# One-core attention, FFN and scan kernel: startup in order of need, weight tasks moved in the first FFN step, rope's turned half in PSUM, identity transposes ahead of the first input

## The chip, the core and the metric

The kernel runs on one core of a Trainium2 chip. The core has a matrix engine (TensorE, here PE; loading its stationary operand is listed apart, as PEld), VectorE (DVE), ScalarE (ACT), GpSimd (POOL) and a queue engine for transfers (SyncE, SP). They run side by side and wait for each other through semaphores. SBUF is the working memory; PE writes its results to PSUM, eight banks of 128 x 512 floats. The metric is the device time in microseconds, the median of several runs.

## What is computed

x is 4 x 512 x 256 floats. Four residual layers follow each other, each on the layer norm of x:

```
x = x + attention(layernorm(x))     # latent attention, 16 heads, causal
x = x + ffn(layernorm(x))
x = x + scan(layernorm(x))          # linear recurrence over 512 steps
x = x + ffn(layernorm(x))           # the same weights again

attention: q_c = rms(x @ wq_down.T) * q_norm_w         # 192 wide
           kv_c = rms(x @ wkv_down.T) * kv_norm_w      # 64 wide
           q = [q_c @ wq_up.T, rope(q_c @ wq_rope.T)]  # 128 + 64 per head
           k = [(kv_c @ wkv_up.T)[:128], rope(x @ wk_rope.T)]
           out = softmax(mask(q k.T * scale)) @ v @ wo.T
rope:      o1 = x1*cos - x2*sin;  o2 = x1*sin + x2*cos
ffn:       w = lut[idx]  (16 values);  down(silu(gate(x)) * up(x))
scan:      xp = x @ W_in.T; dt = softplus(xp @ W_dt.T + b); y_t = exp(-dt*exp(log_A)) * y_(t-1) + xp_t
```

## The kernel before

Every engine has its own program, written out by hand; there is no scheduler. Matrices that need full precision are split into a high and a low part (`_hi`, `_lo`), and a product is three matmuls (`split_mm`, L615 to L617). ACT writes the high part of a PSUM bank, DVE the low part.

*Weight tasks.* `TASKS` is a list of small steps (semaphore to wait for, count, functions for PE, ACT and DVE, PSUM bank). `pe_tasks`, `act_tasks` and `dve_tasks` run a range of it; a task's bank is free when DVE is done with its last user. D tasks transpose the `down` weights, N tasks multiply `wqu` by `wkn` into `wa`/`wb` (this folds the up projection of q with that of k, L294), R tasks transpose the rope weights into the same tensors (L306), W tasks transpose `wo` (L316), V tasks multiply it by the value weights into `wo_a`/`wo_b` (L373; "v-output tasks"), G tasks transpose the FFN's gate and up weights, S and the last L task prepare the scan's weights, the first three L tasks transpose `w_dn`. POOL builds the FFN weights from the 16-value table in chunks of `GC` columns, one comparison (L746) and one addition (L752) for each value, and raises `lut_sum`.

*Startup (batch 0).* DVE takes the statistics of x, normalises it to `xn`; PE transposes it (L580); `down` projects it per tile of 128 tokens; ACT copies each tile to `cd` and takes squares (`down_copy`, L778, L784); DVE runs `token_step` 0 to 23: root of the mean square, scaling of q (L1061), scaling of kv, rope of k. `to_features` (L1444) transposes `cd` in three blocks (q's first 128 columns, its last 64, and k), which ACT and DVE split (`feature_high`, `feature_low`).

*Attention loop.* A unit is four heads of one tile of 128 queries, 16 units a batch, 64 in all. Work is pipelined in slots: slot s runs `q_up` of unit s (L1459 to L1463, bank 0), `q_transpose` of unit s-2, scores of units s-2 and s-3, transposes of probabilities and products with values of s-4 and s-5, and the output projection of s-6. On DVE, `rope_q` of unit s reads bank 0: the product with cos goes to `q_tok` (L1111), the turned half times sin to `q_rot` (L1113, L1114), and L1116 adds them. The first 8 slots (`LEAD`) of batch 0 have nothing of an earlier batch beside them; W and V tasks follow slots 0 to 2 there (`early_tasks`), and after slot 1 DVE takes the statistics of batches 1 to 3 (`at_stats_of`) and normalises batch 1.

*FFN and scan.* Eight steps of 512 tokens follow (each batch once for each FFN layer); the first (`pe_first`, `act_first`, `dve_first`) has the remaining weight tasks between its gate/up tiles.

## Time and profile before

| | |
|---|---|
| Median of 3 runs | 856.2 us (856.1 to 857.96) |
| Profiled execution | 857.25 us, span 855.2 us |
| Busy share of the span | PE 89%, PEld 76%, DVE 79%, ACT 71%, POOL 59% |
| Chain that ended last | PE 59%, DVE 15%, ACT 12%, issue 12% |
| PE clock by 1/40 of the span | full, but for slices 2 and 4 (0.7 and 0.6) and slice 30 (0.8) |

A row of the timeline gives start, duration, engine, line, tiles and, in brackets, the idle time before it and what ended it. Matmul durations overlap: the distance between starts is the rate. The granted clock is 1.00 at 2.4 GHz and 0.50 at 1.2 GHz. Busy shares are means over stages with different limits, so stages are read one by one.

### The profile page before, as it was taken

How to read it: one execution, taken by the hardware profiler on the slowest of the kernel's cores; microseconds unless marked ns; L12 is line 12 of the kernel's file. 1: busy time of each engine (PE TensorE's matmuls, PEld its weight loads, DVE VectorE, ACT ScalarE, POOL GpSimd, SP SyncE). 2: the span in 40 equal slices, each digit the busy share in tenths (PEclk: the TensorE clock that was granted, in tenths of full speed). 3: DMA queues.
4: the chain of work that ended last, by engine and by line, in shares of the span. 5: the costliest groups of instructions: out<-in, count | busy, mean ns of one | idle time of the engine just before them, and what ended most of it. 6: DMA issues, size and time to landing. Idle time of an engine off the chain costs nothing.

```text
span 855.2 us, 15308 instructions
## 1 busy us (share of the span) xinstructions
PE 763.8 (89%) x4556; PEld 652.6 (76%) x4556; DVE 677.6 (79%) x2216; ACT 610.7 (71%) x1500; POOL 503.2 (59%) x543
## 2 busy tenths in 40 slices
PE   4767988898989899998899999999898999999998
PEld 3656767787877687876777888877787887887987
DVE  3676879898879999888989899896756778777643
ACT  2455888888888888888888899996515575665232
POOL 0599999999999999999999999981000000000000
PEclk9796999999999999999999999999989999999999
DMA  9800000000000000000000100000000000000000
GB/s 245 256 1 1 1 1 2 1 2 2 2 1 2 1 1 2 2 1 2 1 2 1 38 2 1 2 1 1 1 1 1 1 1 2 1 1 25 26 26 25
DMA packets 15377, 14.53 MB, mean 17 GB/s; under 512 B 5792, under 2 KB 14432, under 8 KB 15040
## 3 DMA queue, kind: packets, MB, share of 16 engines
q1 hardware_dynamic: 13792, 11.41, 4.6%
q0 software_dynamic: 624, 2.12, 0.8%
q8 instruction: 37, 0.61, 0.3%
q14 instruction: 44, 0.36, 0.1%
q10 hardware_dynamic: 880, 0.04, 0.1%
HBM read 11.46 MB, written 2.10 MB: 16 GB/s over the span
## 4 chain that ended last, share of the span: by engine, by line
PE 59%; DVE 15%; ACT 12%; issue 12%; DMA 0%; DVEq 0%; SPq 0%; ACTq 0%
PE bank L615 12%; PE bank L617 11%; PE bank L616 11%; PE bank L1496 4%; ACT prob L798 4%; ACT prob L818 3%; PE bank L1510 2%; PE bank L1513 2%; DVE pt_lo L1149 2%; ACT pt_hi L827 2%; PE bank L1523 2%; PE bank L580 2%; PE bank L1525 2%; DVE bias_m L1097 1%; PE bank L1470 1%
## 5 line engine op out<-in xcount | busy, mean ns | idle before, releaser
L746 POOL TENSOR_SCALAR hot<-raw_gu,lut 128x256 f32<-128x256 int32 x165 | 192.9, 1169 | 16.7
L752 POOL TENSOR_TENSOR total<-total,hot 128x256 f32<-128x256 f32 (+1 forms) x238 | 172.9, 726 | 19.9
L1097 DVE CUSTOM_DVE_ANT_0 bank<-bank,mask 128x128 f32<-128x128 f32 (+3 forms) x256 | 126.1, 493 | 38.6 <-issue 36.5
L798 ACT ACTIVATE prob<-bank,bias_m 128x128 f32<-128x128 f32 (+3 forms) x256 | 136.1, 532 | 23.9 <-DVE bias_m L1097 23.2
L1149 DVE TENSOR_TENSOR pt_lo<-bank,pt_hi 128x512 fp32r<-128x512 f32 x160 | 108.9, 681 | 10.2 <-ACT pt_hi L827 10.0
L1496 PE MATMUL bank<-ident,prob 128*128 128x128 f32 x640 | 98.6, 277 | 14.9 <-ACT prob L818 10.3
L818 ACT ACTIVATE prob<-prob,rden 128x128 f32<-128x128 f32 (+3 forms) x224 | 105.4, 536 | 6.0 <-DVE rden L1132 5.5
L615 PE MATMUL bank<-kt_hi,qt_hi 128*128 128x128 f32 (+3 forms) x256 | 89.6, 350 | 19.8 <-DVE xt_lo L589 5.0
L827 ACT CAST pt_hi<-bank 128x512 fp32r<-128x512 f32 x160 | 93.5, 585 | 13.9 <-PE bank L1513 8.8
L746 POOL TENSOR_SCALAR hot<-raw_dn,lut 128x256 f32<-128x256 int32 (+1 forms) x90 | 97.2, 1080 | 9.1
L1496 PEld LDWEIGHTS bank<-ident,prob 128*128 128x128 f32 x640 | 72.9, 140 | 31.9 <-ACT prob L818 16.7
L616 PE MATMUL bank<-kt_lo,qt_hi 128*128 128x128 f32 (+3 forms) x256 | 83.1, 325 | 0.0
L617 PE MATMUL bank<-kt_hi,qt_lo 128*128 128x128 f32 (+3 forms) x256 | 83.1, 324 | 0.0
L615 PEld LDWEIGHTS bank<-kt_hi,qt_hi 128*128 128x128 f32 x256 | 48.9, 191 | 35.7 <-DVE xt_lo L589 7.7
L1510 PE MATMUL bank<-pt_hi,v_hl 128*128 128x512 f32 x160 | 68.6, 429 | 5.1 <-issue 4.3
L901 ACT ACTIVATE silu<-bank 128x512 f32<-128x512 f32 x40 | 24.0, 601 | 67.1 <-PE bank L617 67.1
L615 PE MATMUL bank<-xt_hi,gu_hi 128*128 128x512 f32 (+1 forms) x176 | 70.2, 399 | 1.5 <-DVE h_f L1269 1.5
L617 PE MATMUL bank<-xt_hi,gu_lo 128*128 128x512 f32 (+1 forms) x176 | 69.4, 394 | 0.0
L616 PE MATMUL bank<-xt_lo,gu_hi 128*128 128x512 f32 (+1 forms) x176 | 69.3, 394 | 0.0
L1523 PE MATMUL bank<-wo_a,o_a 128*128 128x256 f32 x256 | 68.2, 299 | 0.1
L1525 PE MATMUL bank<-wo_b,o_b 128*128 128x256 f32 x256 | 63.7, 281 | 0.0
L1513 PE MATMUL bank<-pt_lo,v_hl 128*128 128x512 f32 x160 | 63.2, 395 | 0.3 <-DVE pt_lo L1149 0.2
(207 smaller groups left out, 2103.0 us busy)
## 6 DMA issues: line engine op xcount, KB each, us to landing
x<-in_L_attn_a_x_dram SPq DMA_DIRECT2D x4, 512.0 KB, 7.3
wo_nat<-in_L_attn_a_wo_dram SPq DMA_DIRECT2D x1, 2048.0 KB, 13.6
out_dram<-x SPq DMA_DIRECT2D x16, 128.0 KB, 1.8
wqu<-in_L_attn_a_wq_up_dram SPq DMA_DIRECT2D x2, 768.0 KB, 9.0
wqr<-in_L_attn_a_wq_rope_dram SPq DMA_DIRECT2D x4, 192.0 KB, 7.3
raw_dn<-in_L_ffn_down_idx_dram POOLq DMA_DIRECT2D x1, 688.0 KB, 10.1
raw_gu<-in_L_ffn_gate_idx_dram POOLq DMA_DIRECT2D x1, 640.0 KB, 7.4
raw_gu<-in_L_ffn_up_idx_dram POOLq DMA_DIRECT2D x1, 640.0 KB, 7.9
```

Source lines behind the costliest of these rows:

```text
L615: nc.tensor.matmul(o, l_hi, r_hi, start=start and k == 0, stop=False)
L616: nc.tensor.matmul(o, l_hi, r_lo, start=False, stop=False)
L617: last = nc.tensor.matmul(o, l_lo, r_hi, start=False, stop=stop and k == n - 1)
L746: nc.gpsimd.tensor_scalar((hot if v else total)[:, 0:n], raw[:, c:c + n], float(v), lut[:, v:v + 1], ALU.is_equal, ALU.mult).then_inc(lut_ ...
L752: nc.gpsimd.tensor_tensor(dst, total[:, 0:n], hot[:, 0:n], ALU.add).then_inc(lut_sum, 1)
L798: nc.scalar.activation(prob[:, n % 2, h, 0:w], bank[2 + h % 2][:, 0:w], ACT.Exp, bias=bias_m[:, n % 2, h:h + 1], scale=-1.0, accum_out=den ...
L818: nc.scalar.activation(prob[:, n % 2, h, 0:w], prob[:, n % 2, h, 0:w], ACT.Copy, scale=rden[:, n % 2, h:h + 1]).then_inc(norm_a, 1)
L827: nc.scalar.copy(pt_hi[:, c % 2, :, :].rearrange("p h d -> p (h d)"), bank[4 + c % 2][:, :])\
L1097: nc.vector.tensor_tensor_reduce(out=bank[2 + h % 2][:, 0:w], in0=bank[2 + h % 2][:, 0:w], in1=mask[:, TB * P - w:TB * P], scale=1.0, scal ...
L1149: nc.vector.tensor_tensor(pt_lo[:, c % 2, :, :].rearrange("p h d -> p (h d)"), bank[4 + c % 2][:, :], pt_hi[:, c % 2, :, :].rearrange("p h ...
L1496: last = nc.tensor.transpose(bank[4 + c % 2][:, h * P:(h + 1) * P], prob[:, n % 2, h, j * P:(j + 1) * P], ident[:, :])
L1510: nc.tensor.matmul(bank[6][:, :], v, pt_hi[:, c % 2, :, :].rearrange("p h d -> p (h d)"), start=j == 0, stop=False)
```

## The change

- PE transposes the identity 32 times into bank 0 while it waits for `xn`, and 8 times after the D tasks.
- The N and R tasks are ordered by half: the four that heads 0 to 7 need, then (after slot 0's `q_up`) the other four. All four `down` tiles come before them. The first two feature blocks are made before the kv scaling and the rope of k.
- The statistics of batches 1 to 3 are dealt out behind the V tasks (12 `bn_stats`), in slot 3 (aggregation and root) and in slot 4 (normalisation). The transposes of `xn` of batch 1 move to slots 4 and 5, bank 7.
- `q_rot` is gone from SBUF: the turned half is written over the first 64 columns of each head in bank 0. `q_up` waits for all four operations of the unit before it, not for three.
- `GC` is 352 columns in place of 256.
- In the first FFN step the `w_dn` tasks come before the scan's; the last scan task (`t_dt_in`) is run inside `ffn_down`, between its two pairs of tiles.

```diff
+WARM = 32
...
-        GC = GT * DIM // 11
+        GC = GT * DIM // 8
...
+        R_TASKS = [(qr_dup, 1, t_rope(p, k), 4 + p) for k in range(2) for p in range(2)]
+        Q_TASKS = N_TASKS[0:2] + R_TASKS[0:2] + N_TASKS[2:4] + R_TASKS[2:4]
...
+        L_TASKS = [(lut_sum, gu_sums + dn_sums, t_dn(k), 4 + k) for k in range(3)]
+        S_TASKS = [(ssm_in, 64, t_wdt(), 7), (ssm_in, 64, t_ssm(0), 2), (ssm_in, 64, t_ssm(2), 3),
+                   (ssm_in, 64, t_dt_in(), 2)]
+        TASKS = D_TASKS + Q_TASKS + W_TASKS + V_TASKS + G_TASKS + L_TASKS + S_TASKS
...
+        def rest_stats(k):
+            e, tiles = nc.vector, slice(TB, BATCH * TB)
+            if k < REST_TILES:
+                if k % TB == 0:
+                    e.wait_ge(x_in_s[1 + k // TB], 16)
+                e.bn_stats(at_stats[:, TB + k, :], x[:, TB + k, :]).then_inc(at_bn, 1)
+            elif k == REST_TILES:
+                e.wait_ge(at_bn, BATCH * TB)
+                settle(2 * G)
+                for t in range(TB, BATCH * TB):
+                    e.bn_aggr(at_mv[:, t, :], at_stats[:, t, :]).then_inc(at_agg, 1)
+                e.wait_ge(at_agg, BATCH * TB)
+                e.tensor_scalar(at_v[:, tiles], at_mv[:, tiles, 1], LN_EPS, None, ALU.add).then_inc(at_ref, 1)
+            else:
+                rsqrt_step(k - REST_TILES - 1, at_ref, RSQRT + 2, at_v[:, tiles], at_r[:, tiles], at_t[:, tiles])
         def at_norm(p, t):
...
+                turned = heads(bank[0])[:, :, 0:KR]
...
-                nc.vector.tensor_tensor(q_rot[:, :, 0:half], raw[:, :, half:ROPE], s0, ALU.mult).then_inc(q_rope, 1)
-                nc.vector.tensor_tensor(q_rot[:, :, half:ROPE], raw[:, :, 0:half], s1, ALU.mult).then_inc(q_rope, 1)
+                nc.vector.tensor_tensor(turned[:, :, 0:half], raw[:, :, half:ROPE], s0, ALU.mult).then_inc(q_rope, 1)
+                nc.vector.tensor_tensor(turned[:, :, half:ROPE], raw[:, :, 0:half], s1, ALU.mult).then_inc(q_rope, 1)
                 dve.wait_ge(q_rope, k + 3)
-                nc.vector.tensor_tensor(q, q, q_rot[:, :, :], ALU.add).then_inc(q_rope, 1)
+                nc.vector.tensor_tensor(q, turned, q, ALU.add).then_inc(q_rope, 1)
...
+            def early_dve(k0, k1):
+                for k in range(k0, k1):
+                    dve_tasks(dve, k, k + 1)
+                    if V0 <= k < G0:
+                        for j in range(REST_TILES * (k - V0) // (G0 - V0), REST_TILES * (k + 1 - V0) // (G0 - V0)):
+                            rest_stats(j)
...
+                    if b == 0 and s == 3 and k <= RSQRT:
+                        rest_stats(REST_TILES + k)
+                    if b == 0 and s == 4 and k < TB:
+                        at_norm(1, k)
+                    if b == 0 and s in (4, 5) and k == 11:
+                        dve_xt_part(1, s - 4, bank[7])
...
+            for k in range(1 + RSQRT + TB):
+                token_step(k, 0)
             dve.wait_ge(qn_ready, 2)
-            dve_tasks(dve, N0, N0 + 2)
+            dve_tasks(dve, N0, N1)
+            feature_low(0, 0)
+            feature_low(0, 1)
             dve.wait_ge(tables_in, 16 * 3)
-            for k in range(TOKEN_STEPS):
+            for k in range(1 + RSQRT + TB, TOKEN_STEPS):
                 token_step(k, 0)
-            dve_tasks(dve, N0 + 2, W0)
-            for k in range(3):
-                feature_low(0, k)
+            dve_slot(0, 0, None, (N1, W0))
+            feature_low(0, 2)
             split_values(0)
             dve.wait_ge(a_exp, 1)
             nc.vector.tensor_scalar(a_neg[:, :], a_neg[:, :], -1.0, None, ALU.mult).then_inc(a_ready, 1)
-            for s in range(LEAD):
+            early_dve(*early_tasks(0))
+            for s in range(1, LEAD):
                 dve_slot(s, 0, None, early_tasks(s))
-                if s == 1:
-                    for b in range(1, BATCH):
-                        dve.wait_ge(x_in_s[b], 16)
-                    at_stats_of(1, BATCH)
-                    for t in range(TB):
-                        at_norm(1, t)
-                if s == 3:
-                    dve_xt(1)
             for b in range(BATCH - 1):
                 for s in range(LEAD, UNITS + LEAD):
                     dve_slot(s, b, b + 1)
...
             pe.wait_ge(ident_in, 16)
+            for k in range(WARM):
+                nc.tensor.transpose(bank[0][:, k % 4 * P:(k % 4 + 1) * P], ident[:, :], ident[:, :])
             pe_xt(0)
             pe_tasks(pe, D0, N0)
+            for k in range(WARM // 4):
+                nc.tensor.transpose(bank[0][:, k % 4 * P:(k % 4 + 1) * P], ident[:, :], ident[:, :])
             def down(b, t):
...
-                free_after(pe, q_rope, 4 * (b * UNITS + n) - 1)
+                free_after(pe, q_rope, 4 * (b * UNITS + n))
...
-            down(0, 0)
-            down(0, 1)
-            pe_tasks(pe, N0, N0 + 1)
-            for t in (2, 3):
-                pe.wait_ge(dp_cp, t - 1)
+            for t in range(TB):
+                if t >= 2:
+                    pe.wait_ge(dp_cp, t - 1)
                 down(0, t)
-            pe_tasks(pe, N0 + 1, W0)
-            pe.wait_ge(prep_act, W0)
-            pe.wait_ge(prep_dve, W0)
-            pe.wait_ge(sq, 2 * TB)
+            pe_tasks(pe, N0, N1)
+            pe.wait_ge(prep_act, N1)
+            pe.wait_ge(prep_dve, N1)
+            pe.wait_ge(tok, 1 + TB)
+            to_features(0, 0)
+            to_features(0, 1)
+            pe_slot(0, 0, None)
+            pe_tasks(pe, N1, W0)
             pe.wait_ge(tok, 1 + 12)
-            for k in range(3):
-                to_features(0, k)
-            for s in range(LEAD):
-                if s == 5:
-                    wait_xt(pe, 1)
+            to_features(0, 2)
+            pe_tasks(pe, *early_tasks(0))
+            for s in range(1, LEAD):
+                if s == 2:
+                    pe.wait_ge(prep_act, W0)
+                    pe.wait_ge(prep_dve, W0)
                 if s == 6:
                     pe.wait_ge(prep_act, G0)
                     pe.wait_ge(prep_dve, G0)
                 pe_slot(s, 0, None)
                 pe_tasks(pe, *early_tasks(s))
-                if s == 3:
+                if s == 4:
                     pe.wait_ge(prep_dve, G0)
-                    pe_xt(1)
+                if s in (4, 5):
...
-            def ffn_down(k, si):
+            def ffn_down(k, si, inside=None):
                 for pair in range(0, TB, 2):
+                    if pair and inside is not None:
+                        inside()
                     if pair and si is not None:
                         pe.wait_ge(sp_act, 4 * si + 2)
...
-                pe_tasks(pe, G0 + 4, S0)
+                pe_tasks(pe, G0 + 4, L0)
                 weights(G0 + 4)
                 gate_up(0, 2)
                 gate_up(0, 3)
-                pe_tasks(pe, S0, S0 + 2)
-                weights(S0)
+                pe_tasks(pe, L0, L0 + 2)
+                weights(L0)
                 gate_up(0, 4)
-                pe_tasks(pe, S0 + 2, L0 + 1)
+                pe_tasks(pe, L0 + 2, S0 + 1)
                 gate_up(0, 5)
-                pe_tasks(pe, L0 + 1, L1)
-                weights(L0 + 3)
+                weights(L0 + 2)
                 pe_xt(ffn_xt(1))
-                weights(L1)
-                ffn_down(0, None)
+                pe.wait_ge(hf_s, FT)
+                pe_tasks(pe, S0 + 1, S1 - 1)
+                weights(S0 + 1)
+                ffn_down(0, None, lambda: pe_tasks(pe, S1 - 1, S1))
             pe_first()
+            weights(S1)
             for k in range(1, STEPS):
```

ACT's program is reordered in the same way. The transfers and their order are unchanged.

Line numbers in the rows of the changed kernel are its own; there `down` is L635 to L637, `to_features` L1482, `q_up` L1497 to L1501, the xn transposes L600.

PE's program at startup, before, from the last `down` matmul on (`wkn`, `wqu`: N tasks; `wqr`: R tasks; `cd`: `to_features`; `wo_nat`: W tasks):

```order
L617 MATMUL bank<-down_hi,xt_lo 128x320
L294 MATMUL bank<-wkn,wqu 128x64 x24
L306 MATMUL bank<-ident,wqr 128x128 x16
L1444 MATMUL bank<-ident,cd 128x128 x4
L1444 MATMUL bank<-ident,cd 64x128 x4
L1444 MATMUL bank<-ident,cd 128x128 x4
L1459 MATMUL bank<-wa_hi,qa_hi 128x512
L1460 MATMUL bank<-wa_lo,qa_hi 128x512
L1461 MATMUL bank<-wa_hi,qa_lo 128x512
```

and in the changed kernel, from its last `down` matmul on:

```order
L637 MATMUL bank<-down_hi,xt_lo 128x320
L294 MATMUL bank<-wkn,wqu 128x64 x16
L306 MATMUL bank<-ident,wqr 128x128 x8
L1482 MATMUL bank<-ident,cd 128x128 x4
L1482 MATMUL bank<-ident,cd 64x128 x4
L1497 MATMUL bank<-wa_hi,qa_hi 128x512
L1498 MATMUL bank<-wa_lo,qa_hi 128x512
L1499 MATMUL bank<-wa_hi,qa_lo 128x512
L1500 MATMUL bank<-wb_hi,qb_hl 128x512
L1501 MATMUL bank<-wb_lo,qb_hl 128x512
L294 MATMUL bank<-wkn,wqu 128x64 x16
L306 MATMUL bank<-ident,wqr 128x128 x8
```

The first `q_up` (five matmuls with `wa` and `wb`) has moved ahead of half of the N and R tasks and of the third feature block.

DVE's program at the V tasks (`wo_b`: the V tasks' low part; `at_stats`: statistics of batches 1 to 3; `qt_lo`: unit 0), before:

```order
L383 TENSOR_TENSOR wo_b<-bank,wo_a 64x512 x3
L1121 TENSOR_TENSOR qt_lo<-bank,qt_hi 128x512
L524 BN_STATS at_stats<-x 128x6 x12
L498 MEMSET scratch 128x1
L528 BN_AGGR at_mv<-at_stats 128x2 x12
L531 TENSOR_SCALAR at_v<-at_mv 128x12
L507 TENSOR_SCALAR at_t<-at_v 128x12
L509 TENSOR_SCALAR at_r<-at_t 128x12
```

and in the changed kernel:

```order
L383 TENSOR_TENSOR wo_b<-bank,wo_a 64x512
L544 BN_STATS at_stats<-x 128x6
L383 TENSOR_TENSOR wo_b<-bank,wo_a 64x512
L544 BN_STATS at_stats<-x 128x6 x2
L383 TENSOR_TENSOR wo_b<-bank,wo_a 64x512
L544 BN_STATS at_stats<-x 128x6
L1142 TENSOR_TENSOR qt_lo<-bank,qt_hi 128x512
L383 TENSOR_TENSOR wo_b<-bank,wo_a 64x512
L544 BN_STATS at_stats<-x 128x6 x2
L383 TENSOR_TENSOR wo_b<-bank,wo_a 64x512
L544 BN_STATS at_stats<-x 128x6
L383 TENSOR_TENSOR wo_b<-bank,wo_a 64x512
```

The twelve statistics stood in one piece behind three of the eight V tasks; now one or two stand behind each.

PE's program at the end of the first FFN step, from the last matmul of the last gate/up tile (112 rows) on (`w_dn`: the L tasks; `wdt_t`: `t_dt_in`; `xn`: the next step's input; `dn_hi`, `h_hi`: `ffn_down`), before:

```order
L617 MATMUL bank<-xt_hi,gu_lo 112x512
L414 MATMUL bank<-ident,w_dn 128x128 x6
L414 MATMUL bank<-ident,w_dn 48x128 x2
L363 MATMUL bank<-wdt_t,ssm_nat 128x256 x4
L580 MATMUL bank<-ident,xn 128x128 x8
L615 MATMUL bank<-dn_hi,h_hi 128x256
L616 MATMUL bank<-dn_lo,h_hi 128x256
```

and in the changed kernel:

```order
L637 MATMUL bank<-xt_hi,gu_lo 112x512
L600 MATMUL bank<-ident,xn 128x128 x8
L331 MATMUL bank<-ident,ssm_nat 128x128 x8
L635 MATMUL bank<-dn_hi,h_hi 128x256
L636 MATMUL bank<-dn_lo,h_hi 128x256
L637 MATMUL bank<-dn_hi,h_lo 128x256
```

The `w_dn` transposes have gone from here to earlier gate/up tiles, the input of the next step stands right behind the last tile, and `t_dt_in` is no longer ahead of `ffn_down`.

## Rows read from the trace of the kernel before

**Rows 1.** stretches: us; busy us of PE, PEld, DVE, ACT, POOL (instructions); clock, DMA, GB/s

```profile
80.00:592.00 512.00, 466.07 (x2876) 395.02 (x2875) 452.63 (x1576) 445.35 (x1203) 456.28 (x487) 1.00 0.01 3
592.00:633.00 41.00, 36.95 (x215) 32.53 (x214) 25.65 (x65) 17.57 (x33) 0.00 (x0) 0.92 0.00 1
```

**Rows 2.** a DMA issue, then the timeline to 50 us: start, us, engine, line, tiles

```profile
ident<-in_ident_dram SPq DMA_DIRECT2D x1, 64.0 KB, 1.8
...
10.90 1.94 PE L580 MATMUL bank<-ident,xn 128*128 128x128 f32 x8 [10.90 <-DVE xn L543]
...
15.61 0.60 PE L615 MATMUL bank<-down_hi,xt_hi 128*128 128x320 f32 x1 [1.13 <-DVE down_lo L275]
...
23.55 0.41 ACT L778 COPY cd<-bank 128x320 f32<-128x320 f32 x1
...
24.64 0.19 ACT L784 ACTIVATION_READ_ACCUMULATOR squares<-cd 128x1 f32 x1
...
26.35 0.16 DVE L1056 TENSOR_SCALAR rms_v<-ms 128x8 f32<-128x8 f32 x1
...
28.81 1.01 DVE L1061 TENSOR_SCALAR cd<-cd,rms_r 128x192 f32<-128x192 f32 x4
...
31.84 0.74 DVE L283 SCALAR_TENSOR_TENSOR wa_lo<-bank,qn_a,wa_hi 128x512 fp32r<-128x512 f32 x1
...
35.98 2.79 PE L1444 MATMUL bank<-ident,cd 128*128 128x128 f32 x12 [1.80 <-issue]
...
39.40 0.76 PE L1459 MATMUL bank<-wa_hi,qa_hi 128*128 128x512 f32 x1 [0.62 <-ACT kt_hi L791]
...
49.37 2.83 PE L373 MATMUL bank<-wo_t,wv 128*128 128x256 f32 x12 [1.77 <-DVE wo_t L324]
```

**Rows 3.** a stretch of one microsecond, and the timeline of PE in it

```profile
43.00:44.00 1.00, 1.00 (x7) 1.00 (x6) 0.89 (x3) 0.51 (x2) 0.90 (x2) 0.52 0.00 0
...
41.67 3.90 PE L316 MATMUL bank<-ident,wo_nat 128*128 128x128 f32 x24
```

**Rows 4.** timeline, 55 to 73 us, DVE, ACT and PE

```profile
55.34 4.01 DVE L524 BATCH_NORM_STATS2 at_stats<-x 128x6 f32<-128x256 f32 x12
...
57.00 0.59 ACT L379 CAST wo_a<-bank 128x512 fp32r<-128x512 f32 x1 [2.02 <-PE bank L373]
...
66.00 2.47 DVE L383 TENSOR_TENSOR wo_b<-bank,wo_a 64x512 fp32r<-64x512 f32 x4
...
70.11 0.68 DVE L383 TENSOR_TENSOR wo_b<-bank,wo_a 64x512 fp32r<-64x512 f32 x1 [1.65 <-ACT wo_b L380]
...
72.32 0.73 PE L1459 MATMUL bank<-wa_hi,qa_hi 128*128 128x512 f32 x1
```

**Rows 5.** who waited for `q_rot`; the addition's durations and group; two pairs of the timeline

```profile
  PE bank L1459: 2.3, 7
...
L1116 DVE TENSOR_TENSOR q_tok<-q_tok,q_rot x64: 424/426/992, 43.2 to 562.3; 128x256 f32<-128x256 f32 x64
...
L1116 DVE TENSOR_TENSOR q_tok<-q_tok,q_rot 128x256 f32<-128x256 f32 x64 | 33.0, 516 | 2.2
...
84.77 0.28 DVE L1114 TENSOR_TENSOR q_rot<-bank,sin 128x128 f32<-128x128 f32 x1
...
85.20 0.47 PE L1459 MATMUL bank<-wa_hi,qa_hi 128*128 128x512 f32 x1
...
497.82 0.28 DVE L1114 TENSOR_TENSOR q_rot<-bank,sin 128x128 f32<-128x128 f32 x1
...
498.25 0.47 PE L1459 MATMUL bank<-wa_hi,qa_hi 128*128 128x512 f32 x1
```

**Rows 6.** timeline of PE, 618 to 628 us, idle time before in brackets

```profile
618.89 1.06 PE L580 MATMUL bank<-ident,xn 128*128 128x128 f32 x8 [1.82 <-issue]
...
621.71 0.55 PE L615 MATMUL bank<-dn_hi,h_hi 128*128 128x256 f32 x1 [1.75 <-issue]
...
627.61 0.30 PE L615 MATMUL bank<-dn_hi,h_hi 128*128 128x256 f32 x1
```

97 lines of the change are left out of this document (48 added, 49 removed).

## The prediction

> **What bounds the kernel now.** I read the stretches first, then the timeline of the two where TensorE (PE) is not full, then the waits around `q_up` in the attention loop. In the long attention part, 80 to 592 us, PE is busy 466 of 512 us and VectorE (DVE) 453, ScalarE (ACT) 445: three engines near full that hand work round a loop [rows 1]. So a saved microsecond of PE alone is worth little there, and a longer step in the loop can cost all of itself. Outside the loop it is different: the first FFN step (592 to 633) has PE busy 37 of 41 us, with waits in one place [rows 1, 6], and before 80 us each engine waits for the others in turn [rows 2 to 4].
>
> **The change part by part.** The profiled execution took 857.25 us (span 855.2, 2.05 around it); the median of the plain runs is 856.2. I sum against 857.25 and take 1.05 off at the end.
>
> *Prologue order, up to the first v-output task.* Before, the first `q_up` starts at 39.40, because the feature transposes (35.98) wait until all eight `wa`/`wb` tasks and the whole token chain are through DVE [rows 2]. After, they wait for four tasks and for the first half of the token chain. Built from durations of the rows: the PE clock is assumed up when x is normalised (below), so the first `down` starts at about 14.1 in place of 15.61 (14 transposes of 1.94 us per eight, half of it saved, less what ACT's copies keep). All four `down` tiles follow each other, and ACT paces them: one tile is 23.55 to 24.83, 1.28 us. First tile ready at 15.1, so the squares end at 15.1 + 4 x 1.28 = 20.2 (before 24.83). DVE then does the 12 small steps and four scalings, 26.35 to 29.82, that is 3.5 us: 23.7. Four `wa`/`wb` halves at 0.74 us each, overlapping to 0.66: 26.4. `to_features` for two of three blocks, and from its start to the first `q_up` 39.40 - 35.98 = 3.4: 29.9. That is 9.5 us earlier. What was deferred now lies between this `q_up` and the first v-output task (49.37): before that took 10.0 us; the four further `wa`/`wb` tasks and their matmuls add the 2.7 us of DVE and about 0.9 us in which PE and ACT fill the pipe: 13.6, so 43.5. Term: 43.5 - 49.37 = **-5.9**. DVE, and not PE, is the engine that is late here. The transfers do not stop it: by 43 us nothing is moved any more [rows 3], and the spread statistics read x from about 44 on.
>
> *Statistics of batches 1 to 3 spread out.* Before, DVE runs 12 `BATCH_NORM_STATS2` (55.34, 4.01 us) and then aggregates, takes the root and normalises until 66.0, 10.7 us in one piece, while its `wo_b` splits wait, and DVE finishes the last split at 70.11 + 0.68 = 70.79 [rows 4]. From 49.37 that is 21.4 us. After, the stats are interleaved with the eight tasks. ACT then paces: two casts of 0.59 us each per task, 8 x 1.2 = 9.6, with a `qt_hi` and a `q_tok` copy between them (1.0), PE's lead before the first cast (about 1.1) and one last split (0.7): 12.4 us. A stat and a half beside each split is 0.6 + 0.6 us of DVE in 1.2 us of ACT, so it is hidden; if not, it would cost up to 4.0. Term: **-9.0**. The other 66.0 - 59.35 = 6.7 us of DVE work comes back in slots 3 and 4, where `rest_stats` and `at_norm` sit between the parts. DVE had room there before, since PE ran slow (a `q_up` matmul took 0.73 us at 72.32, against 0.47 at 85.20 [rows 4, 5]). Bounds 0 and 6.7; I take **+1.9**, as DVE work per slot and the room nearly balance in slot 3 and not in slot 4. Prologue in all: -13.0, with bounds of -17 and -8.
>
> *Warm transposes.* The identity lands about 2.9 us in (issue at 0.72 plus 0.38, 1.8 to land), and eight cold transposes take 1.94 us, so 32 take at most 7.8 us and end by 10.7, before PE's first input at 10.90 [rows 2]. At about 43.98 the clock rose from 1.2 to 2.4 GHz when PE had been running a `q_up` and then transposes without pause since 39.40, and the last 2.1 us of that were transposes of `wo_nat` [rows 2, 3]. I read that as transposes counting as activity. The eight after the `down` weight tasks are then about 0.9 us beside ACT's and DVE's splits. Against it: the transposes of xn and of the `down` weights ran from 10.90 to 14.48 (1.13 before 15.61) and the first `down` matmul still took 0.60. If the clock doesn't rise, `down` starts at 14.48 + 8 x 0.24 = 16.4 instead of 14.1, and its tiles are paced by PE at 1.6 us (six matmuls 0.27 apart): 16.4 + 6.4 + 1.3 = 24.1, 3.9 later. The Trainium skill, "TensorE: Matmul & The Clock Gate", part 4 on PE-mode transposes, says that a transpose doesn't count as PE-busy in the same way and that the full clock doesn't engage for it; by that rule the warm transposes are idle load and this second case is the one that comes about. The trace has a row for either reading.
>
> *Rope's turned half in PSUM.* The last addition reads PSUM and SBUF instead of two SBUF tiles. Its 64 instances took 33.0 us, 516 ns on average, while the shortest took 424, which I take as the price without interference: at best 64 x 0.09 = 5.9 us of DVE less [rows 5]. But the halves now stand in bank 0, so `q_up` of the next unit must wait for the fourth operation and not for the third. DVE is just ahead of PE there: the second half ends at 85.05 and `q_up` starts at 85.20; at 498.10 and 498.25 the same 0.15 us. Of the 59 units from unit 5 on, 36 start within 0.35 us of that end; these two are the first and the last of them [rows 5]. The addition ends about 0.46 us after it, so these `q_up` come up to 0.45 us later. Full price 36 x 0.45 = 16.2 us; gain if none passes -5.9. The trace puts only 2.3 us over 7 times down to this wait [rows 5]; yet the chain of waits, followed through these slots, runs over `q_up` in about half of them. Half of the first (8) less half of the second (3): **+5**. Behind the waiting `q_up` on PE stand the scores of head 3, which DVE's last row maximum and ACT's exp wait for.
>
> *Larger chunks on GpSimd (256 to 352 columns).* GpSimd's table sums were done before the first FFN step (GpSimd is busy 0.00 us in 592 to 633 [rows 1]), so nobody waits for them. Fewer, longer instructions end earlier and leave DVE undisturbed at the end: **-1**, between -3 and +1.
>
> *First FFN step.* PE waits 1.82 us before the transposes of xn (618.89) and 1.75 us before `ffn_down` (621.71), because `dn_lo` and the last `ssm_lo` come late on DVE. After that pause the clock is at 1.2 GHz until 627.61: 27 matmuls in 5.90 us, that is 0.22 us each, and about 0.12 at 2.4 GHz [rows 6]. After, the `w_dn` tasks stand two gate tiles earlier, xn follows the last gate tile without a wait, and the `wdt`-times-`w_in` task, before `ffn_down` so far, stands inside it, with the same work. Gain 1.82 + 1.75 - 0.2 for a shorter wait on `h_f`, and 2.6 for the slow stretch: **-6.0**, between -3.4 (clock drops all the same) and -7. PE sets the pace after that, so it stays. Late next is `h_f` of the last tile.
>
> Sum: -13.0 - 6.0 + 5 - 1 = -15.0. 857.25 - 15.0 - 1.05 = 841.2, so 841 us.
>
> **Rivals.**
> 1. *The rope wait is absorbed.* For it: the trace books only 2.3 us to it, and DVE saves up to 5.9. Against it: PE and DVE are both near 90% busy, so there is little slack. Then the term is -3 in place of +5: 833.
> 2. *The clock doesn't rise on transposes.* The prologue gives 3.9 us less: 845. For it: after 3.6 us of transposes the first `down` matmul ran slow. Against: the rise during `wo_nat`'s transposes. (This is where the rule of the Trainium skill named above leads.)
> 3. *DVE is the bound of slots 3 to 5.* All 6.7 us come back, and the stats aren't hidden (4.0): 841 + 4.8 + 4.0 = 850. For it: DVE has the work in either order. Against: while PE waited for it in the old block, ACT and PE were the ones idle, and with the block gone DVE gets their time.
> 4. *Slower than before.* The mechanism is the q_up wait alone. If each of the 64 units is lengthened, by the wait for the addition and by slower writes to PSUM, the gains elsewhere (20.0 us) are used up from 20.0 / 64 = 0.31 us a unit on. At 0.45 us the term is 64 x 0.45 = 29, and the time 856.2 - 20.0 + 29 = 865. Against it: 23 of 59 units have more than 0.35 us to spare, and DVE's part gets shorter.
>
> **How the numbers follow.** Forecast (838 to 844) 0.44; rival 1 0.22; rival 2 0.15; rival 3 0.12; rival 4 0.04; something that leaves the time where it is, 0.03. The range reaches from a rope gain with a full prologue, 830, to rival 3, 850; outside it lie about 2 in 10. A measurement tells about 0.2% (1.7 us) from no change. Faster by more: 0.93; within: 0.03; slower: 0.04.
>
> **What the profile would show.** Right: the first `q_up` near 30 and the first v-output matmul near 43; no PE pause of 7 us between v-output tasks; `ffn_down` straight behind the transposes with the clock at full level; `q_up` starting some 0.15 us after the addition in most units, and the stretch between the eighth unit and the last scores about 4 us longer. Wrong: `down` not before 16 and its matmuls 0.27 us apart, as at 1.2 GHz; slots 3 and 4 longer than 7.5 us each; an unchanged or shorter attention loop, which would say that the wait is absorbed.

## The result and the profile after

The changed kernel takes 867.2 us (median of 4 runs, 865.55 to 869.07) against 856.15 us before: a ratio of 1.013, 95% interval 1.010 to 1.016. It is slower; the forecast was 841 us, 830 to 850. A few executions lay far outside the others of the same kernel (885.76, 2376.35, 2546.01 and 4090.15 us); they are in no ratio.

First the page of the changed kernel, busy tenths and granted clock in 40 slices:

```profile
span 865.5 us, 15232 instructions
PE   7777988898888898898899899999998999999998
PEclk9695999999999999999999999999999999999999
```

Then the two long stretches, the attention loop and the first FFN step (us; busy us of PE, PEld, DVE, ACT, POOL; clock, DMA, GB/s), to be read beside [rows 1]:

```profile
80.00:605.00 525.00, 469.04 (x2866) 395.29 (x2865) 452.08 (x1572) 445.49 (x1199) 409.83 (x340) 0.99 0.01 3
605.00:645.00 40.00, 37.98 (x229) 32.26 (x229) 28.40 (x70) 18.66 (x35) 0.00 (x0) 1.00 0.00 1
```

The loop does the same work (469 us of PE, 452 of DVE) in 525 us in place of 512. The FFN step runs wholly at 2.4 GHz now, 0.92 before. The clock's row shows the startup at 0.6 and 0.5 in slices 2 and 4, where the kernel before has 0.7 and 0.6. In slice 1 the row is no guide: it reads full in the kernel before, although `down`'s first twelve matmuls start 0.27 us apart there (15.61 to 18.68) and its last twelve 0.15 us (21.18 to 22.88). Up to the first change that the row shows, the durations tell the clock.

The timeline of PE to 51 us (start, us, engine, line, tiles, wait before it), for [rows 2]:

```profile
2.91 6.59 PE L1463 MATMUL bank<-ident 128*128 128x128 f32 x32 [2.91 <-DMA ident<-in_ident_dram]
...
10.96 1.09 PE L600 MATMUL bank<-ident,xn 128*128 128x128 f32 x8 [1.46 <-DVE xn L563]
...
14.50 0.38 PE L635 MATMUL bank<-down_hi,xt_hi 128*128 128x320 f32 x1 [0.43 <-DVE down_lo L275]
...
27.44 1.94 PE L1482 MATMUL bank<-ident,cd 128*128 128x128 f32 x8 [4.58 <-DVE wb_lo L283]
30.85 0.76 PE L1497 MATMUL bank<-wa_hi,qa_hi 128*128 128x512 f32 x1 [1.48 <-DVE qb_hl L1109]
...
33.12 6.92 PE L294 MATMUL bank<-wkn,wqu 128*128 128x64 f32 x32
39.84 1.91 PE L306 MATMUL bank<-ident,wqr 128*128 128x128 f32 x8
...
50.18 2.83 PE L373 MATMUL bank<-wo_t,wv 128*128 128x256 f32 x12 [1.78 <-DVE wo_t L324]
```

Up to the first `q_up` the forecast holds: `down` at 14.50 (forecast 14.1), feature transposes 27.44 (26.4), `q_up` 30.85 (29.9), 8.6 us earlier than before. Then everything is lost. From this `q_up` to the first v-output matmul it is 19.3 us, where the forecast had 13.6 and the kernel before 10.0. The four deferred tasks' 32 matmuls take 6.92 us, 0.22 us each, where the same kind took 0.114 before. The eight feature transposes took 1.94 us, the level of 1.2 GHz, and stand behind a wait of 4.58 us. The first v-output task starts at 50.18, 0.8 us later than before.

The same kernel in the V tasks and slots 3 to 5 (timeline of PE and DVE), for [rows 4]:

```profile
55.93 0.67 DVE L1142 TENSOR_TENSOR qt_lo<-bank,qt_hi 128x512 fp32r<-128x512 f32 x1
...
56.70 0.45 PE L635 MATMUL bank<-kt_hi,qt_hi 128*128 128x128 f32 x1 [2.08 <-issue]
...
57.37 5.86 PE L373 MATMUL bank<-wo_t,wv 128*128 128x256 f32 x20
...
67.66 0.48 PE L635 MATMUL bank<-kt_hi,qt_hi 128*128 128x128 f32 x1 [3.69 <-ACT prob L818]
...
77.42 0.77 PE L1497 MATMUL bank<-wa_hi,qa_hi 128*128 128x512 f32 x1 [1.21 <-DVE q_tok L1137]
...
80.76 1.38 DVE L563 TENSOR_SCALAR xn<-x,at_mv,at_r 128x256 f32<-128x256 f32 x3
...
87.16 0.54 PE L1497 MATMUL bank<-wa_hi,qa_hi 128*128 128x512 f32 x1
```

No 7 us pause is left, but there are pauses of 2.08 us (1.73 at the same place before) and 3.69 us, and the `q_up` at 77.42 still has matmuls of 0.77 us. The granted clock is 0.50 from 68 to 86 us; in the kernel before it was from 66 to 78. Starts of `q_up` by unit (from the timelines):

| unit | before | after |
|---|---|---|
| 0 | 39.40 | 30.85 |
| 3 | 72.32 | 68.65 |
| 5 | 85.20 | 87.16 |
| 8 | 102.04 | 104.86 |
| 63 | 553.69 | 571.35 |

So 2.8 us are lost by unit 8, and 14.8 us between units 8 and 63 (466.49 us against 451.65). What lies behind unit 63 is 7.4 us shorter.

A timeline is one execution, and startups differ. In six timelines with the same order of the startup and no warm transposes (the kernel before and five of the runs below) the first `q_up` starts between 39.30 and 42.04 and the first v-output matmul between 49.23 and 51.62. Differences of 2 us at the start of a single timeline are therefore not evidence by themselves.

Rope in the changed kernel, for [rows 5]: who waited (us in total, times, longest), and the group of the addition (count, busy us, mean ns, idle before):

```profile
PE bank L1497 <- DVE q_tok L1137: 14.5, 31, 1.5
```

```profile
L1137 DVE TENSOR_TENSOR q_tok<-bank,q_tok 128x256 f32<-128x256 f32 x64 | 27.2, 425 | 2.2
```

The addition got as short as forecast (33.0 us to 27.2), and the wait for it went from 2.3 us over 7 times to 14.5 over 31.

The end of the first FFN step, for [rows 6]:

```profile
630.90 1.03 PE L600 MATMUL bank<-ident,xn 128*128 128x128 f32 x8
633.27 1.09 PE L331 MATMUL bank<-ident,ssm_nat 128*128 128x128 f32 x8 [1.34 <-DVE h_f L1300]
634.12 0.36 PE L635 MATMUL bank<-dn_hi,h_hi 128*128 128x256 f32 x1
```

The wait before xn is gone, one of 1.34 us (for `h_f`, "late next" in the prediction) is left, and `ffn_down` runs at 0.12 us a matmul from its start.

### The profile page after: what moved, and what is told of

The parts are those of the page before. It is cut to its first block, busy times and chain, and to the rows that moved or that the text cites. A ratio compares the mean times of both kernels' runs of the same rounds, so it can differ in the third digit from the quotient of the medians.

```text
span 865.5 us, 15232 instructions
## 1 busy us (share of the span) xinstructions
PE 775.4 (90%) x4596; PEld 659.3 (76%) x4596; DVE 677.8 (78%) x2216; ACT 611.7 (71%) x1500; POOL 458.3 (53%) x388
## 4 chain that ended last, share of the span: by engine, by line
PE 56%; DVE 18%; issue 14%; ACT 11%; DMA 0%; DVEq 0%; SPq 0%; ACTq 0%
PE bank L635 11%; PE bank L637 11%; PE bank L636 10%; PE bank L1534 4%; ACT prob L838 3%; DVE pt_lo L1170 3%; ACT prob L818 2%; PE bank L1548 2%; PE bank L1551 2%; PE bank L1563 2%; DVE bias_m L1117 2%; PE bank L1565 2%; PE bank L1497 2%; DVE o_b L1176 2%; ACT pt_hi L847 1%
## 5 line engine op out<-in xcount | busy, mean ns | idle before, releaser
L766 POOL TENSOR_SCALAR hot<-raw_gu,lut 128x352 f32<-128x352 int32 x120 | 176.6, 1472 | 12.2
L772 POOL TENSOR_TENSOR total<-total,hot 128x352 f32<-128x352 f32 (+1 forms) x168 | 157.7, 938 | 14.0
L635 PE MATMUL bank<-kt_hi,qt_hi 128*128 128x128 f32 (+3 forms) x256 | 90.1, 352 | 22.3 <-DVE xt_lo L609 5.3
L766 POOL TENSOR_SCALAR hot<-raw_dn,lut 128x352 f32<-128x352 int32 (+1 forms) x60 | 87.0, 1450 | 6.1
L637 PE MATMUL bank<-kt_hi,qt_lo 128*128 128x128 f32 (+3 forms) x256 | 83.8, 327 | 0.0
L635 PEld LDWEIGHTS bank<-kt_hi,qt_hi 128*128 128x128 f32 x256 | 49.4, 193 | 38.2 <-DVE xt_lo L609 8.0
L635 PE MATMUL bank<-xt_hi,gu_hi 128*128 128x512 f32 (+1 forms) x176 | 70.2, 399 | 1.6 <-DVE h_f L1300 1.5
L637 PE MATMUL bank<-xt_hi,gu_lo 128*128 128x512 f32 (+1 forms) x176 | 69.4, 394 | 0.0
## 6 DMA issues: line engine op xcount, KB each, us to landing
wo_nat<-in_L_attn_a_wo_dram SPq DMA_DIRECT2D x1, 2048.0 KB, 12.4
```

The costliest lines, as they stand in the source:

```text
L635: nc.tensor.matmul(o, l_hi, r_hi, start=start and k == 0, stop=False)
L637: last = nc.tensor.matmul(o, l_lo, r_hi, start=False, stop=stop and k == n - 1)
L766: nc.gpsimd.tensor_scalar((hot if v else total)[:, 0:n], raw[:, c:c + n], float(v), lut[:, v:v + 1], ALU.is_equal, ALU.mult).then_inc(lut_ ...
L772: nc.gpsimd.tensor_tensor(dst, total[:, 0:n], hot[:, 0:n], ALU.add).then_inc(lut_sum, 1)
```

## The experiments

Each ratio is against the kernel before, timed beside it on the same chip, with a 95% interval; "us" is the ratio less one times 855. Theory at this point: rope's wait costs its full price in the loop, and the prologue's gain is given back because TensorE falls to 1.2 GHz in its waits. Rivals: the parts cost something by themselves (GpSimd's chunks, PSUM writes), or deferred tasks are slow for another reason.

### Rope alone, and its wait alone

```diff
-                nc.vector.tensor_tensor(q, q, q_rot[:, :, :], ALU.add).then_inc(q_rope, 1)
+                nc.vector.tensor_tensor(q, turned, q, ALU.add).then_inc(q_rope, 1)
...
-                free_after(pe, q_rope, 4 * (b * UNITS + n) - 1)
+                free_after(pe, q_rope, 4 * (b * UNITS + n))
```

> The kernel before with rope's turned half in bank 0 (and q_up waiting for the fourth rope operation), nothing else. Theory A (the chain of the loop runs over q_up in nearly every unit, so the extra operation between the last read of bank 0 and q_up costs its 0.3 us a unit in full): the changed kernel's stretch from unit 8 to unit 63 was 466.5 us against 451.65, so here too 13 to 17 us more, 869 to 873 us. Rival B (my forecast's term, half of it absorbed): +5, 861 us. Rival C (the longer loop of the changed kernel comes from another part of the change, such as GpSimd's longer instructions): 856 to 858 us.

Measured 866.74 us, ratio 1.0135 (1.0112 to 1.0159): +11.5 us. Theory A, a little below its range. The loop from unit 8 to 63 took 463.8 us, against 451.65. Its waits, and one pair of its timeline:

```profile
PE bank L1460 <- DVE q_tok L1117: 13.9, 33, 1.0
```

```profile
85.10 0.42 DVE L1117 TENSOR_TENSOR q_tok<-bank,q_tok 128x256 f32<-128x256 f32 x1
...
85.67 0.47 PE L1460 MATMUL bank<-wa_hi,qa_hi 128*128 128x512 f32 x1 [0.40 <-DVE q_tok L1117]
```

The same `q_up` started at 85.20 in [rows 5]: 0.47 us later, 0.15 us behind the addition's end, as forecast.

```diff
-                free_after(pe, q_rope, 4 * (b * UNITS + n) - 1)
+                free_after(pe, q_rope, 4 * (b * UNITS + n))
```

> The kernel before, with q_rot in SBUF as it was; only q_up waits for the fourth rope operation in place of the third. It tells the wait from the place of the operands. Theory A (the wait is the whole cost): the same as with the turned half in PSUM or slightly above it, since the addition here takes 516 ns on average and there 424: 869 to 877 us. Rival B (the wait is absorbed, the PSUM operand or writes cost the time): 856 to 859 us.

Measured 869.04 to 871.75 us, ratio 1.0175 (1.0149 to 1.0200): +15.0 us. There is no timeline of it to read. The wait is the whole cost. The PSUM operand by itself gives some 3.5 us back (15.0 less 11.5; the two intervals overlap), which is what the addition's 5.8 us of DVE were worth, less whatever the writes to PSUM cost.

### The changed kernel without rope

```diff
-                nc.vector.tensor_tensor(q, turned, q, ALU.add).then_inc(q_rope, 1)
+                nc.vector.tensor_tensor(q, q, q_rot[:, :, :], ALU.add).then_inc(q_rope, 1)
...
-                free_after(pe, q_rope, 4 * (b * UNITS + n))
+                free_after(pe, q_rope, 4 * (b * UNITS + n) - 1)
```

> The changed kernel with the rope part undone (q_rot in SBUF, at the end of the region, q_up waits for the third operation), chunks of 352 columns kept. Theory A: 867.2 less 13 to 17 us: 850 to 854 us, because the first FFN step's gain (7.4 us in the trace) is then no longer covered and the prologue's net is about +2. Rival B (rope is worth 5): 862 us. Rival C (the longer loop is not rope's): 866 to 868 us.

Measured 857.05 us, ratio 1.0027 (0.9999 to 1.0055). Against the changed kernel's 1.0130 that is 8.8 us less. Its loop took 453.5 us in an execution of 853.38 us, 3.7 under the run's median, so the loop of a median execution may well be longer. The run missed the expected 850 to 854: without rope the rest of the change does not gain either. Something beside rope costs some 4 us more than I had it.

### The first FFN step alone

> The kernel before with only the order of the first FFN step changed (w_dn tasks earlier, the input transposes straight behind the last gate tile, the wdt task inside ffn_down). Theory A (this term was right, the two traces differ by 7.4 us behind unit 63, of which some 1 us is GpSimd's): 6 to 7.5 us faster, 849 to 850 us. Rival B (the gain behind unit 63 comes mostly from GpSimd's larger chunks, which end earlier): 2 us or less, 854 to 856 us.

(Its edit is the part of the change's diff from `L_TASKS` on that concerns the first FFN step, in all three engines.) Measured 850.88 us, ratio 0.9951 (0.9932 to 0.9970): -4.2 us. Its timeline shows the same two things as the changed kernel's, xn without a wait and `ffn_down` at full clock:

```profile
616.67 1.09 PE L331 MATMUL bank<-ident,ssm_nat 128*128 128x128 f32 x8 [1.31 <-DVE h_f L1268]
617.51 0.36 PE L615 MATMUL bank<-dn_hi,h_hi 128*128 128x256 f32 x1
```

From the last `q_up` to the second input transposes it is 87.2 us in the kernel before, 85.6 in the rope-alone run (the same FFN code; there the slow clock behind the pause lasted 3.1 us, not 5.9), 81.6 here and 81.1 in the changed kernel. The other timelines agree: 85.6 to 87.2 us in the seven with the old order of this step, 81.0 to 82.0 in the nine with the new one. So the gain is 4 to 6 us, depending on how long the slow clock would have lasted.

### The three parts of the prologue, each alone

Warm transposes:

```diff
             pe.wait_ge(ident_in, 16)
+            for k in range(WARM):
+                nc.tensor.transpose(bank[0][:, k % 4 * P:(k % 4 + 1) * P], ident[:, :], ident[:, :])
             pe_xt(0)
             pe_tasks(pe, D0, N0)
+            for k in range(WARM // 4):
+                nc.tensor.transpose(bank[0][:, k % 4 * P:(k % 4 + 1) * P], ident[:, :], ident[:, :])
```

> The kernel before with only the identity transposes on TensorE added (32 ahead of its first input, 8 behind the down weights). The changed kernel's trace shows full clock for the first xn transposes (1.09 us for eight, 1.94 before). If that is what the transposes do by themselves: xn transposes from 10.9 at full clock, first `down` near 14.5 in place of 15.6, and then at most 1.1 us, since ScalarE's copies and VectorE's token chain pace what follows: 854 to 855.5 us. Rival (the Trainium skill, 'TensorE: Matmul & The Clock Gate', part 4, by which transposes leave the clock low): eight more cold transposes ahead of `down`, 0.8 to 2 us later: 856 to 858 us.

Measured 853.49 us, ratio 0.9979 (0.9956 to 1.0002): -1.8 us, an interval that just takes in no change.

```profile
11.02 1.34 PE L581 MATMUL bank<-ident,xn 128*128 128x128 f32 x8 [1.92 <-DVE xn L544]
...
15.35 0.39 PE L616 MATMUL bank<-down_hi,xt_hi 128*128 128x320 f32 x1
...
47.60 2.83 PE L374 MATMUL bank<-wo_t,wv 128*128 128x256 f32 x12 [1.77 <-DVE wo_t L325]
```

The transposes raised the clock: `down` runs at 0.31 us a matmul at once (0.47 without them, from a first one of 0.60 in [rows 2]). In between the clock had fallen once more: PE stood idle for 1.92 us ahead of the xn transposes, of which the last ran at half rate, the six of `dn_nat` took 1.84 us (1.16 in the changed kernel), and the granted clock is 0.50 in 12 to 14 us. The eight transposes behind them then brought it back. The first v-output task comes 1.8 us earlier, more than the 1.1 us I allowed.

Statistics spread over the V tasks (on VectorE; TensorE and ScalarE take the next input's transposes in slots 4 and 5):

```diff
-                if s == 1:
...
-                    at_stats_of(1, BATCH)
-                    for t in range(TB):
-                        at_norm(1, t)
+                    if b == 0 and s == 3 and k <= RSQRT:
+                        rest_stats(REST_TILES + k)
+                    if b == 0 and s == 4 and k < TB:
+                        at_norm(1, k)
```

> The kernel before with only the statistics and the normalisation of the next batches spread over the v-output tasks and slots 3 to 5. Theory A (the work comes back in slots 3 to 5, where VectorE and the slow clock decide, as in the changed kernel, whose q_up of units 3 to 8 come at 68.65, 77.42, 87.16 to 104.86 against 72.32, 79.70, 85.20 to 102.04): fourth q_up 3 to 5 us earlier, that of unit 8 within 1.5 us of 102.0; 855 to 857 us. Rival B (my forecast, -9.0 + 1.9): 848 to 850 us. Rival C (it costs by itself what the changed prologue loses): 858 to 860 us.

Measured 855.29 us, ratio 0.9995 (0.9970 to 1.0020): -0.4 us. The `q_up` of units 3, 4, 5 and 8:

```profile
66.28 0.73 PE L1483 MATMUL bank<-wa_hi,qa_hi 128*128 128x512 f32 x1
...
74.54 0.76 PE L1483 MATMUL bank<-wa_hi,qa_hi 128*128 128x512 f32 x1 [0.74 <-DVE q_rot L1132]
...
83.49 0.73 PE L1483 MATMUL bank<-wa_hi,qa_hi 128*128 128x512 f32 x1
...
101.25 0.40 PE L1483 MATMUL bank<-wa_hi,qa_hi 128*128 128x512 f32 x1
```

Unit 3 is 6.0 us earlier than the 72.32 of before, unit 8 only 0.8. The gain is real and comes back in slots 3 to 5, of which 3 and 4 take 8.3 and 9.0 us (7.4 and 5.5 before), at matmuls of 0.73 to 0.76 us (1.2 GHz). Theory A, with more gained by unit 3 than its 3 to 5 us.

The V tasks themselves, from their first matmul to VectorE's last split, took 14.7 us (49.40 to 64.09), where the forecast had 12.4 and the kernel before 21.4. The difference is a wait that [rows 4] did not make visible: PE stands 2.09 us before unit 0's scores (1.73 in the kernel before), and ScalarE's casts behind it stand 2.38.

The order up to the first v-output task:

```diff
-            pe_tasks(pe, N0 + 1, W0)
...
+            pe_tasks(pe, N0, N1)
...
+            to_features(0, 0)
+            to_features(0, 1)
+            pe_slot(0, 0, None)
+            pe_tasks(pe, N1, W0)
```

> The kernel before with only the order up to the first v-output task changed (four down tiles first, four wa/wb tasks, two feature blocks, the first q_up, then the other four tasks). Theory A (the four deferred tasks run at 1.2 GHz, 6.92 us for 32 matmuls in the changed kernel against 0.114 us each at 2.4 GHz before, so what the first q_up gains is lost again before the first v-output task): first q_up near 32, first v-output matmul 50 to 52, and 856 to 858.5 us. Rival B (my forecast's -5.9 less what the warm clock was worth in it): 850 to 853 us.

Measured 855.16 us, ratio 1.0002 (0.9977 to 1.0026): +0.2 us.

```profile
33.13 0.77 PE L1466 MATMUL bank<-wa_hi,qa_hi 128*128 128x512 f32 x1 [1.48 <-DVE qb_hl L1092]
...
35.40 6.92 PE L294 MATMUL bank<-wkn,wqu 128*128 128x64 f32 x32
...
52.79 2.83 PE L373 MATMUL bank<-wo_t,wv 128*128 128x256 f32 x12 [2.34 <-DVE wo_t L324]
```

The first `q_up` is 6.3 us earlier, the first v-output task 3.4 us later, and the 6.92 us are there again without the warm transposes. The median is a little below theory A's 856 to 858.5 and above rival B's 850 to 853; the profiled execution has it as A says. Of the 3.4 us, up to 2.3 can be the spread of startups (49.23 to 51.62 with the old order).

### GpSimd's chunks

```diff
-        GC = GT * DIM // 11
+        GC = GT * DIM // 8
```

The changed kernel with 256 columns (`// 11`):

> The changed kernel with GpSimd's chunks at 256 columns as before. It gives the price of the larger chunks within the change. Theory A (nobody waits for GpSimd; VectorE's additions beside it are 0.42 us in either case now that the addition reads PSUM): 867 to 868.5 us, 1 us at most above the changed kernel. Rival B (chunks of 352 hold VectorE up longer and are part of the loop's growth): 862 to 865 us.

Measured 864.46 us, ratio 1.0103 (1.0071 to 1.0136), against the changed kernel's 1.0130: 2.3 us less (the intervals overlap), loop 463.7 against 466.5. Rival B's side. And the kernel before with 352 columns:

> The kernel before with only GpSimd's chunks at 352 columns. With and without rope, going back to 256 columns made the changed kernel faster: ratio 1.0130 to 1.0103, and 1.0027 to 0.9978. Theory A (longer GpSimd instructions hold VectorE's SBUF operations up for longer, and the loop pays): 1 to 3 us slower, 856 to 858 us, the loop from unit 8 to 63 1.5 to 2.5 us longer than 451.65. Rival B (my forecast's -1; the two differences were scatter): 853.5 to 855.5 us.

Measured 861.04 us, ratio 1.0065 (1.0036 to 1.0095): +5.6 us, beyond theory A's 3. In its profiled execution unit 8 comes 1.9 us later, which is within the spread of startups, and the loop takes 455.2 us, 3.6 more. DVE is busy for 405.5 us of it, in place of 400.5, with the same work. Groups of DVE in 105 to 540 us (count, busy us, mean ns, idle before), of the kernel before and then of this one:

```profile
L1061 DVE TENSOR_SCALAR cd<-cd,rms_r 128x192 f32<-128x192 f32 x12 | 4.6, 384 | 0.1
...
L515 DVE SCALAR_TENSOR_TENSOR rms_r<-rms_t,rms_r 128x8 f32<-128x8 f32 x9 | 2.7, 301 | 0.0
...
L513 DVE SCALAR_TENSOR_TENSOR rms_t<-rms_t,rms_v 128x8 f32<-128x8 f32 x9 | 1.6, 177 | 0.1
```

```profile
L1061 DVE TENSOR_SCALAR cd<-cd,rms_r 128x192 f32<-128x192 f32 x12 | 5.5, 462 | 0.1
...
L513 DVE SCALAR_TENSOR_TENSOR rms_t<-rms_t,rms_v 128x8 f32<-128x8 f32 x9 | 3.6, 402 | 0.1
...
L515 DVE SCALAR_TENSOR_TENSOR rms_r<-rms_t,rms_r 128x8 f32<-128x8 f32 x9 | 2.5, 276 | 0.0
```

One operation on 8 columns that reads two SBUF tiles (L513) takes 402 ns on average in place of 177, and once 922 ns; the longest rope addition went from 0.99 to 1.22 us. GpSimd's own instructions are 1488 and 946 ns long in place of 1171 and 749. Such DVE work seems to stand until the GpSimd instruction ends, and a longer one holds it longer. The other timelines confirm L513 (341 to 402 ns in the three with 352 columns, 162 to 285 in the thirteen with 256), but not every operation: L515, of the same kind and size, takes 276 in place of 301, and L1061's 384 to 462 lies close to what timelines with 256 columns reach (416). So single operations are a weak measure here; the sum over the loop (5.0 us more) is the better one.

By the Trainium skill, "SBUF — State Buffer", section "Who interferes with whom", the two engines share a port pair which whoever starts first keeps for its whole instruction, and an operation with two SBUF inputs wants it too; the rows of L513 and of the addition agree, that of L515 shows no effect. That this holding is what lengthens the loop is argued from them, not shown by a run of its own. Against it stands that without rope the loop is no longer with 352 columns (453.5 us, in an execution faster than its median) than with 256 (453.8, in the next section).

### The prologue's parts together, and the clock held up

Prologue and FFN step alone are left when the changed kernel is taken without rope and with 256 columns:

> The changed kernel without its rope part and without the larger GpSimd chunks: prologue and first FFN step alone. Parts measured by themselves: FFN -4.2, warm transposes -1.5, spread +0.3, order +0.2. Theory A (the prologue's parts disturb each other: at unit 8 the changed kernel is 2.1 to 2.8 us late, the parts alone sum to -0.8): FFN -4.2 and prologue +2.5, 852.5 to 854.5 us with the kernel before at 855. Theory B (the parts add up, and the larger chunks were what cost): 849 to 850.5 us.

Measured 853.68 us, ratio 0.9978 (0.9956 to 0.9999): -1.9 us. Theory A: the FFN step's -4.2 with +2.3 for the prologue, although its parts by themselves sum to -2.0. Which part disturbs:

> The kernel before with the first FFN step's order, the warm transposes and the spread statistics: all of the change but the prologue's order, rope and the chunks. If the disturbance is between order and warm transposes: the sum of the parts, 849 to 850.5 us. If it is between spreading and the others: 852 to 854 us.

Measured 849.66 us, ratio 0.9939 (0.9915 to 0.9962): -5.2 us. That is all of the kernel above but the changed order, and near the sum of its parts (-6.4). So the order, worth nothing alone, costs 3.3 us in company. The startups show the same: beside the warm transposes the first v-output matmul comes at 50.18 to 51.30 with the new order (four timelines) and at 47.60 and 48.69 with the old one.

Then the same kernel with TensorE kept busy in its waits:

```diff
             pe_tasks(pe, N0, N1)
+            pe.wait_ge(dp_cp, 4)
+            fill(32)
             pe.wait_ge(prep_act, N1)
...
             to_features(0, 1)
+            fill(10)
             pe_slot(0, 0, None)
```

`fill(n)` is n transposes of the identity into bank 3.

> As the kernel above, with 42 identity transposes more on TensorE where it waits: 32 behind the first four wa/wb tasks (4.6 us idle in the changed kernel), 10 ahead of the first q_up (1.5 us idle). Theory A (the deferred tasks are slow because the clock fell in those waits): clock at full level from 11 to 43, the 32 matmuls of the deferred tasks 3.7 us in place of 6.92, first v-output matmul at 45 to 47 in place of 50 to 51, and 3 to 5 us faster than without them. Rival B (something else holds the deferred tasks, such as their semaphores or weights): duration unchanged at 6.9 us and no gain.

Measured 848.69 us, ratio 0.9929 (0.9896 to 0.9962): 4.2 us less than without the filling (5.0 by the medians). The timeline of PE without filling, and with it:

```profile
27.77 1.94 PE L1482 MATMUL bank<-ident,cd 128*128 128x128 f32 x8 [3.65 <-DVE wb_lo L284]
...
33.46 6.92 PE L295 MATMUL bank<-wkn,wqu 128*128 128x64 f32 x32
...
50.48 2.83 PE L374 MATMUL bank<-wo_t,wv 128*128 128x256 f32 x12 [1.77 <-DVE wo_t L325]
```

```profile
22.59 3.66 PE L1615 MATMUL bank<-ident 128*128 128x128 f32 x32
26.84 1.06 PE L1482 MATMUL bank<-ident,cd 128*128 128x128 f32 x8 [0.59 <-issue]
...
30.90 3.68 PE L295 MATMUL bank<-wkn,wqu 128*128 128x64 f32 x32
...
44.63 0.67 PE L374 MATMUL bank<-wo_t,wv 128*128 128x256 f32 x2 [1.76 <-DVE wo_t L325]
...
96.50 0.40 PE L1497 MATMUL bank<-wa_hi,qa_hi 128*128 128x512 f32 x1
```

Work that does nothing made the deferred tasks take 3.68 us in place of 6.92 and brought the first v-output task 5.9 us forward, to 44.63: 1.1 us from my forecast of 43.5. Unit 8 comes at 96.50, 7.1 us earlier than the 103.57 without filling, in an execution that was the fastest of its six (845.93 us). The theory of the clock holds for the deferred tasks, rival B is out. Whether the new order is worth anything once the clock is held up is another question; the section on the best versions answers it.

### What stands behind the waiting `q_up`

```diff
-                do(q_up, s)
                 do(scores, s - 3, 3)
+                do(q_up, s)
```

> The kernel with rope's turned half in PSUM alone, and on TensorE q_up issued one place later in each slot, behind the scores of head 3. Theory A (the wait hurts because the scores of head 3 stand behind the waiting q_up, and the row maximum and exp of head 3 wait for them): most of the 11.7 us comes back, 856 to 860 us. Rival B (the chain runs from q_up through its own results, the q_tok copy and rope of the same unit, or VectorE's order counts): no gain or a loss, 866 to 872 us.

Measured 864.47 us, ratio 1.0115 (1.0067 to 1.0162), within the interval of rope alone, between the two theories' ranges and nearer to B's. The wait itself all but vanished, and another grew:

```profile
PE bank L615 <- ACT prob L798: 13.7, 46, 1.3
...
PE bank L1460 <- DVE q_tok L1117: 1.6, 4, 0.4
```

13.9 us of wait became 1.6 and the time stayed. But PE now stands 13.7 us, in 46 places, before scores that wait for ScalarE's exp (`prob`) to free their bank; with rope alone this wait was 2.9 us in 8 places. The move therefore exchanged one wait for another of the same size. Theory A's gain did not come, and that much is against it. That `q_up`'s own results are the chain, as rival B has it, the run does not show, since the exchanged wait would explain the time as well.

### The best versions

```diff
-            pe_tasks(pe, N0 + 1, W0)
+            pe_tasks(pe, N0 + 1, R0 + 2)
+            pe.wait_ge(dp_cp, 4)
+            fill(24)
+            pe_tasks(pe, R0 + 2, W0)
+            fill(12)
...
                 to_features(0, k)
+            fill(4)
```

> The kernel before with the first FFN step's order, the warm transposes, and 40 further identity transposes where TensorE waits between 27 and 38 us (24 ahead of the last two wa/wb tasks, 12 ahead of the feature transposes, 4 ahead of the first q_up). No change of the prologue's order, no spreading, rope as before. Parts: -4.2 and -1.5; if the clock stays up to 45 us, the 3 feature blocks take 1.6 in place of 2.8, q_up 1.3 in place of 2.3, the wo_nat transposes 3.1 in place of 4.1: 3 us more. 846 to 848 us if the theory of the clock holds, 849 to 850 if it doesn't.

Measured 847.13 us (846.8 to 847.65), ratio 0.9904 (0.9868 to 0.9939): 8.2 us faster than before, as the theory of the clock has it. No run has the FFN step and the warm transposes without the filling; by themselves the two sum to -6.0.

This kernel has the old order of the startup, with the clock held up. Its timeline answers what the new order is worth then. First its own first `q_up` and first v-output matmul:

```profile
35.80 0.47 PE L1466 MATMUL bank<-wa_hi,qa_hi 128*128 128x512 f32 x1 [0.90 <-DVE qb_hl L1089]
...
44.83 2.83 PE L374 MATMUL bank<-wo_t,wv 128*128 128x256 f32 x12 [2.33 <-DVE wo_t L325]
```

With the new order and the filling they came at 29.68 and 44.63. So the new order brings the first `q_up` 6.1 us forward and the first v-output matmul 0.2. What stands between the two takes 15.0 us in place of 9.0, and DVE has the same work up to there in either order (19.3 and 19.4 us busy from 15 us on). It was the filling that gave the date near my forecast of 43.5, not the order. With the statistics spread as well:

> The kernel before with the first FFN step's order, the warm transposes, the filling transposes between 27 and 38 us and the spread statistics: the parts of the change that paid, plus the filling. The version without spreading had 847.1 us (ratio 0.9904). If spreading adds what it did to the warm version (849.7 against an expected 849.3, nothing): 846 to 848 us. If, with the clock up, it gives its saving of the V stretch (3.8 to 6 us earlier at unit 3) and keeps it: 843 to 845 us.

Measured 849.18 us, ratio 0.9925 (0.9900 to 0.9950): -6.4 us, above both of the expected ranges. Spreading doesn't pay with the startup's clock up either: in its profiled execution unit 3 is 3.7 us earlier than without spreading, unit 5 1.8 us later (81.71 against 79.88). The clock was up in the startup only; in slots 3 and 4 it was 0.50 from 64 to 82 us, and no run holds it up there. The kernel with filling and the new order (-6.1, with spreading too) is as fast as this one with the old order, so in the total too the order is worth nothing. The version to keep is the FFN step's order with warm and filling transposes, rope and chunks as before.

## Why the prediction was wrong

By the parts alone: rope +11.5, chunks +5.6, FFN -4.2, warm -1.8, spreading -0.4, order +0.2. They sum to +10.9, and the changed kernel was +11.1. That the sum fits is partly chance: in company the order costs more (3.3), and the chunks perhaps less (2.3 with rope, 4.2 without, neither clear of noise). Against the forecast's -15 the miss is 26 us, and four terms have nearly equal parts in it: rope 6.5, order 6.1, statistics 6.7, chunks 6.6.

- **What bounds the kernel.** Right: in the loop three engines hand work round, and a longer step costs nearly all of itself. I wrote this down and then halved the rope term against it.
- **Rope, +5.** Wrong in size, and its mechanism was right: `q_up` 0.47 us later, addition 0.09 us shorter. The failed step is "half of the first (8) less half of the second (3)". The halving leaned on the 2.3 us over 7 times that the trace put down to this wait. But a wait list counts only idle time that has already opened: in the units where DVE and PE meet within 0.35 us, both are on the path. Full price less what the shorter addition is worth, 16.2 - 3.4 = 12.8, would have been within 1.3 us of the 11.5 measured. My guess of who waits behind it (head 3's scores) found no support: issued ahead of `q_up` they saved nothing, though the new 13.7 us wait leaves the question open.
- **Prologue order, -5.9.** Wrong, +0.2 alone and +3.3 in company. Right to the first `q_up` within 1 us. The failed step is the 13.6 us from there to the first v-output matmul, the deferred tasks as "the 2.7 us of DVE and about 0.9 us in which PE and ACT fill the pipe". It measured 19.3 us: the 32 deferred matmuls alone took 6.92 us behind a wait of 4.58 us, about which I didn't ask what it does to the clock, although I had used the clock's fall behind a pause for the FFN step in the same text. Holding the clock up brings the step to 15.0 us, so the clock is most of the excess. But it does not rescue the term: the 49.37 that I compared with was itself slow (the granted clock was 0.50 from 34 to 44 us), and with its clock held up too the old order has the v-output at 44.83 against 44.63. An earlier first `q_up` is worth nothing here; why the 6 us go between it and the V tasks is not shown, beyond that DVE's work up to there is the same.
- **Statistics, -9.0, and coming back, +1.9.** Wrong in sum: -0.4 in place of -7.1. Of the -9.0, 6.7 came in the V tasks (14.7 us for the 12.4 summed: the sum over ScalarE's casts left out PE's 2.09 us wait before unit 0's scores) and 6.0 by unit 3. What failed is above all the +1.9: 5.2 us of 6.0 came back by unit 8, near its bound of 6.7. "DVE had room there, since PE ran slow" had it the wrong way round, as I read it: with DVE's work between its parts PE stayed at 1.2 GHz for some 20 us in the changed kernel, in place of 14. How much of the 5.2 is DVE's work and how much the clock no run separates.
- **Warm transposes.** Right, though the clock fell again in between in some executions (in the run of the warm transposes alone it did): the clock rose, and the rival by which transposes don't count is refuted (the rule of the Trainium skill, "TensorE: Matmul & The Clock Gate", part 4, doesn't hold for these fp32 transposes of the identity). `down` started at 14.50.
- **GpSimd's chunks, -1.** Wrong in sign and outside the bounds of -3 to +1: +5.6 alone. The failed step is "nobody waits for them", which looked at GpSimd's results only. In the runs DVE is busy 5.0 us longer in a loop that is 3.6 us longer; that GpSimd's instructions hold VectorE's SBUF work is the likely way, not a shown one.
- **First FFN step, -6.0.** Right in mechanism. Measured -4.2 (-5.8 to -2.6), in the traces -4.0 to -6.1; the slow stretch that it removes varies from run to run.
- **The rivals.** Rival 4 named the place, but gave it 0.04 and took the gains elsewhere as 20 us. The loop did grow by 14.8/55 = 0.27 us a unit, below its 0.31 (0.22 with 256 columns); it sufficed because the gains elsewhere weren't there. Rival 3 had the mechanism of slots 3 to 5, with the chance at 0.12. No rival joined two of them. None had GpSimd's longer instructions cost VectorE time, although [rows 5] has additions of 992 ns beside ones of 424, which I had read as interference.

Still open: why the order costs 3.3 us in company and nothing alone; what chain stands behind the waiting `q_up`; and whether the chunks' cost is the held port at all.

## What to carry to other kernels

In a loop where three engines are near 90% busy, price a longer hand-over at full in every unit in which producer and consumer meet closely; a short wait list is no evidence of slack. When work is moved so that TensorE waits some microseconds, price what follows at the lower clock, or fill the wait with transposes of the identity. Price the old order at the same clock as the new one: a term that compares a new order at full speed with an old one that was slow credits the order with what the clock alone would give. VectorE work that is moved between the parts of a slot is not hidden just because another engine is slow there (5.2 of 6.0 us came back), and the length of a GpSimd instruction can be a cost to other engines even where nobody waits for its result.

## What the hardware showed that was not expected

- Transposes of the identity alone raised TensorE's clock from 1.2 to 2.4 GHz: after 32 of them (6.59 us) the eight xn transposes took 1.09 us in place of 1.94 (1.34 in the run of the warm transposes alone, where the clock fell again at once), and 42 in the waits kept it up (3.68 in place of 6.92 us for 32 matmuls).
- After the 4.58 us wait at 22.9 us TensorE stayed at 1.2 GHz until about 43 us, though it was busy without a break from 30.85 on (granted clock 0.50 in every two microseconds from 26 to 42, 0.75 in 42 to 44): a fall cost far more than the wait itself. In the kernel before it came back sooner: PE was busy without a break from 39.40, and the clock was up by 44.
- VectorE's addition of 128x256 took 425 ns on average with one operand in PSUM (never over 427) and 516 with both in SBUF beside GpSimd (up to 992).
- With larger GpSimd instructions (1488 ns in place of 1171) the mean of one 8-column VectorE operation went from 177 to 402 ns, while that of another of the same kind did not grow (301 and 276).
